# A match masked on TensorE and ScalarE in place of VectorE, and loads of a graph kernel asked for earlier

## The chip, the cores and the metric

The kernel runs on one core of one Trainium2 chip. The metric is device time in microseconds (us) of one execution; the lower the better. Five engines work in parallel, each through its own instructions in order, and meet at semaphores: TensorE (PE), VectorE (DVE), ScalarE (ACT), GpSimd (POOL) and SyncE (SP), which here only asks for transfers. A name with q (SPq, ACTq) is an engine's queue of transfer requests.

## The reference

Four graph layers run one after another over 50,000 nodes with 256 features and 50,000 edges, sorted by destination. Each layer normalizes x, rectifies it, lets nodes send messages along edges, and adds the result to x:

```python
edge_index = jnp.stack([src, dst])
h = jnp.maximum(_layernorm(x, axis=-1), 0.0)
x = x + _L0_gnn_ref(h, edge_index, L0_gnn_W, L0_gnn_b, L0_gnn_mag_w, L0_gnn_mag_b, L0_gnn_attn_w)
h = jnp.maximum(_layernorm(x, axis=-1), 0.0)
x = x + _L1_gnn_ref(h, src, dst, edge_weight, L1_gnn_w_nbr, L1_gnn_w_own, L1_gnn_bias)
h = jnp.maximum(_layernorm(x, axis=-1), 0.0)
x = x + _L2_gnn_ref(h, src, dst, L2_gnn_W_s, L2_gnn_W_t, L2_gnn_W_attn, L2_gnn_W_fc, L2_gnn_b_fc)
h = jnp.maximum(_layernorm(x, axis=-1), 0.0)
x = x + _L3_gnn_ref(h, edge_index, edge_attr_2, L3_gnn_W_forward, L3_gnn_W_reverse, L3_gnn_attn_forward)
```

Layer 0 is an attention with a softmax over the edges of a destination; layer 1 a weighted sum; layer 2 an attention with a softmax over the edges of a source, so that it needs the edges in the order of their sources; layer 3 an attention with four heads.

## The kernel before

The program is a row of stages. A stage is a `Phase`: it has its own tiles and semaphores, a block with one body for each engine, and ends with a barrier of all engines (L43), so that no work of a stage overlaps the next one's. The stages that matter here are these.

**Setup.** `constants` (L71) makes identity, ramps and `k.before`, which is 1 where the row index is smaller than the column index. `weights` (L2761) asks for 23 pieces of the weights on SyncE's queue (L2794), waits for all of them, turns them on TensorE and copies them to their places on VectorE. `load_edges` (L99) presets its tiles, asks for 24 pieces of the edge lists on SyncE's queue (L147, L148, L151), waits for all, casts them (L167), and turns them.

**Node stages** (`node_pass`, four of them, one for each layer) go over x in groups of 512 rows: SyncE loads a group, VectorE takes mean and variance and normalizes, TensorE turns and multiplies with weights, ScalarE rectifies and copies. Four buffers of x are set to zero first (L1906), and SyncE waits for that.

**Ranking** (`rank_sources`, L402, once, in layer 0) finds the place of each edge in the order of sources, a counting sort over 392 tiles of 128 edges. A source number is split in a high and a low digit. A first walk makes the histogram. The second walk, the one that the change touches, gives each edge its rank: the start of its bin, plus the earlier tiles' edges with the same key, plus those ahead of it in its own tile. For tile t:

- `head` (VectorE) makes the one-hot of the high digits, `turn` (TensorE) turns the one-hot of the low digits, `copies` (ScalarE) brings it to `low_t`.
- `match` (TensorE) multiplies `low_t` with itself: `p_same` is 1 where two edges of the tile have the same low digit, else 0. `before_in_tile` (VectorE) multiplies it by `k.before` and writes `earlier`.
- `add` (TensorE) adds the tile's counts to the running table `p_run`, in one PSUM bank. `snap` (ScalarE) copies the table to `starts` before each add. Once in eight tiles `coarsen` (VectorE) moves what has gathered to a coarse table, and a second product in `add` (L629) takes it away from `p_run`.
- `rank` (TensorE) makes three products (L647, L648 and, with `earlier`, L651), and `pick` (VectorE) picks the rank.

`walk` writes the stages of an engine's body in a fixed order with lags, the first 16 tiles straight, the others in a hardware loop with eight tiles a turn, in which the numbers to wait for and the addresses are made in registers:

```python
walk(dve, [(0, head), (2, before_in_tile), (3, coarsen), (4, pick)])
walk(pe, [(2, add), (0, turn), (1, match), (3, rank)])
walk(act, [(2, snap), (0, copies)])
```

So in step c ScalarE makes the snap of tile c - 2 and then the copy of tile c; TensorE the add of tile c - 2, the turn of c, the match of c - 1 and the rank of c - 3. A late walk (L589 to L692) follows over the last 168 tiles, with another table. Meanwhile GpSimd gathers rows of h for the edges (L732, L738, L758).

## Time and profile before

| | |
|---|---|
| time, median of 3 runs | 7717.71 us (7708.27 to 7720.84) |
| the profiled execution's own time, and its span | 7719.35 us, 7717.7 us |
| busy: TensorE, VectorE, ScalarE, GpSimd | 75%, 69%, 41%, 50% of the span |
| mean share of the 16 DMA engines | up to 9 tenths in single slices; 202 GB/s over the span |
| setup, up to the end of `load_edges` | 0 to about 54 us |
| ranking stage: histogram, walk, late walk | 672 to 842, 849 to 1374, 1374 to 1535 us |
| first clear of each node stage | 153.2, 2112.9, 3581.4, 6296.8 us |

The span runs from the first to the last instruction. Busy shares are means over stages that have different limits, so that they don't say what a stage waits for. Times in the timeline are counted from the span's start. In it, the matmuls' ends are modelled; their starts, one after another, are the better measure. An idle time in brackets names what ended it; "issue" means that nothing in the profile did.

### The profile page before, as it was taken

To read this page: it belongs to the slowest core of one execution; us is meant where nothing else is said; L and a number is where in the kernel's file an instruction comes from. 1 tells how busy PE (TensorE), PEld (TensorE's weight loads), DVE (VectorE), ACT (ScalarE), POOL (GpSimd) and SP (SyncE) were. 2 spreads that over 40 slices of the span, in tenths; PEclk is the share of its full clock that TensorE was granted. 3 is DMA by queue.
4 is the path that set the end of the run, shared out by engine and by line. 5 is a ranking of instruction groups with operands and counts; after the bars stand their busy time and mean duration, and the time that the engine had idled before them with its cause. 6 is when DMAs were issued, how large, how long until landed. Compare 5 with 4: busy or idle time off the path is not lost. (4 is left out here: it accounts for less than half of the span.)

```text
span 7717.7 us, 154759 instructions
## 1 busy us (share of the span) xinstructions
PE 5751.1 (75%) x23306; PEld 3587.8 (46%) x23307; DVE 5295.3 (69%) x18481; ACT 3154.3 (41%) x8435; POOL 3857.8 (50%) x4924
## 2 busy tenths in 40 slices
PE   4997788967789997677999877778687779400477
PEld 3774333345534444554444355555335668300365
DVE  4999888955589994456666566666784569533765
ACT  1994355214445552344444345455222457300044
POOL 1556777500022224766777677777450013577443
PEclk7998999989999998999999989998899999755799
DMA  1664334469867775797888866666108978422177
GB/s 57 212 210 144 99 103 141 139 197 326 294 226 246 244 246 192 253 308 265 313 315 314 284 199 201 204 204 204 52 25 274 338 250 230 129 55 55 49 238 250
DMA packets 917095, 1560.29 MB, mean 202 GB/s; under 512 B 122254, under 2 KB 633470, under 8 KB 916967
## 3 DMA queue, kind: packets, MB, share of 16 engines
q1 hardware_dynamic: 602758, 860.67, 33.6%
q10 hardware_dynamic: 188000, 410.91, 15.1%
q0 software_dynamic: 126208, 287.39, 13.6%
q14 instruction: 97, 0.79, 0.0%
q8 instruction: 32, 0.52, 0.0%
HBM read 861.12 MB, written 697.48 MB: 202 GB/s over the span
## 5 line engine op out<-in xcount | busy, mean ns | idle before, releaser
L2169 PE MATMUL node_p_out<-w,node_h_t 128*128 128x512 f32 (+2 forms) x6272 | 2174.6, 469 | 18.0 <-ACT node_h_t L2205 16.3
L1473 PE MATMUL merge_banks<-merge_rows,merge_mask 128*128 x6264 | 1523.3, 397 | 541.4 <-DVE merge_mask L1455 161.3
L1473 PEld LDWEIGHTS merge_banks<-merge_rows,merge_mask 128*128 128x128 f32 x6264 | 1184.6, 195 | 880.0 <-issue 723.2
L1455 DVE TENSOR_SCALAR merge_mask<-ramp,dst_at,soft_at_step 128x128 f32<-128x128 f32 x2349 | 824.7, 354 | 770.7 <-PE merge_banks L1473 613.4
L2169 PEld LDWEIGHTS node_p_out<-w,node_h_t 128*128 128x128 f32 x6272 | 1011.6, 190 | 462.8 <-issue 407.2
L2082 POOL TENSOR_TENSOR node_inv_std<-node_var,node_minus_half 128x4 f32<-128x4 f32 x392 | 461.6, 1177 | 1364.5 <-DVE node_var L1967 794.1
L1536 ACT COPY merge_total<-merge_banks 128x1024 f32<-128x1024 f32 x392 | 396.9, 1012 | 1235.7 <-PE merge_banks L1473 1215.8
L2205 ACT ACTIVATE node_h_t<-node_p_turn 128x256 f32<-128x256 f32 x1568 | 602.0, 384 | 199.9 <-PE node_p_turn L2147 194.7
L2147 PE MATMUL node_p_turn<-ident,node_xn 128*128 128x128 f32 x2352 | 466.4, 280 | 130.5 <-DVE node_xn L2038 95.6
L2147 PEld LDWEIGHTS node_p_turn<-ident,node_xn 128*128 128x128 f32 x2352 | 298.4, 141 | 454.5 <-issue 195.8
L2095 POOL DMA_INDIRECT src_sorted<-node_key,node_key_at x392 | 395.6, 1009 | 180.1 <-issue 93.7
L1524 ACT COPY merge_banks<-merge_held 128x1024 f32<-128x1024 f32 x392 | 398.4, 1017 | 193.1 <-PE merge_banks L1463 92.1
L1616 POOL DMA_INDIRECT merge_rows<-h,merge_take_i x408 | 389.5, 955 | 148.4 <-issue 104.7
L2104 POOL TENSOR_TENSOR node_small<-node_small,node_half 128x4 f32<-128x4 f32 x98 | 104.0, 1061 | 711.8 <-ACT node_junk L2184 711.8
L2409 PE MATMUL score_p_h<-w,score_h_t 128*128 128x256 f32 x1568 | 456.1, 418 | 0.1
L2336 POOL DMA_INDIRECT score_b<-to_dst,score_take_b x392 | 376.1, 959 | 119.4 <-issue 119.4
L2334 POOL DMA_INDIRECT score_a<-pair,score_take_a x392 | 377.0, 962 | 104.9 <-issue 90.1
L2546 POOL DMA_INDIRECT score_a<-h,score_take_a x392 | 375.3, 958 | 106.1 <-issue 69.0
L1453 DVE TENSOR_SCALAR merge_mask<-ramp,dst_at 128x128 f32<-128x128 f32 x783 | 297.7, 406 | 173.2 <-PE merge_banks L1473 120.6
L2221 ACT COPY node_out<-node_p_out 128x512 f32<-128x512 f32 x392 | 229.8, 586 | 435.8 <-PE node_p_out L2169 435.8
L2730 PE MATMUL head_rows_p<-ident,head_rows_cols 128*128 128x128 f32 x16 | 3.6, 423 | 523.8 <-DVE head_rows_cols L2718 523.8
L2380 DVE TENSOR_TENSOR score_z<-score_p_a,score_b 128x256 f32<-128x256 f32 x392 | 165.3, 422 | 317.8 <-ACT score_p_a L2470 301.9
(573 smaller groups left out, 11377.0 us busy)
## 6 DMA issues: line engine op xcount, KB each, us to landing
merge_held<-own ACTq DMA_DIRECT2D x196, 512.0 KB, 6.0
x<-merge_total ACTq DMA_DIRECT2D x196, 512.0 KB, 4.5
node_x<-x SPq DMA_DIRECT2D x196, 512.0 KB, 5.0
pair<-node_out SPq DMA_DIRECT2D x98, 1024.0 KB, 4.3
node_x<-in_x SPq DMA_DIRECT2D x194, 512.0 KB, 4.7
merge_rows<-h_by_edge SPq DMA_DIRECT2D x408, 128.0 KB, 3.8
merge_rows<-by_edge SPq DMA_DIRECT2D x408, 128.0 KB, 3.8
h<-node_rows_h SPq DMA_DIRECT2D x98, 516.0 KB, 4.2
```

The source lines that it names most:

```text
L1455: ins = nc.vector.tensor_scalar(mask[j][:], k.ramp[:, 0:P], columns(k.dst_at, s), columns(weight, s), ALU.is_equal, ALU.mult)
L1473: nc.tensor.matmul(banks[:, bass.ds(nc.s_assert_within(at[2 * j + 1], 0, (BANKS - 1) * 512, skip_runtime_bounds_check_because=small), D)], ...
L1524: nc.scalar.copy(four_banks(q), held[q.held][:]).then_inc(seeded, G)
L1536: nc.scalar.copy(total[q.total][:], four_banks(q)).then_inc(kept, G)
L1616: nc.gpsimd.indirect_dma_start(rows[:, (j + n) * D:(j + n + 1) * D], None, table, bass.IndirectOffsetOnAxis(take_i[:, j + n:j + n + 1], 0) ...
L2082: nc.gpsimd.tensor_tensor(inv_std[q.h][:], var[q.h][:], minus_half[:], ALU.pow).then_inc(std_made, 1)
L2095: nc.gpsimd.indirect_dma_start(k.src_sorted, bass.IndirectOffsetOnAxis(key_at[:, g:g + 1], 0), key[:, g:g + 1], None, bounds_check=k.NP - ...
L2147: ins = nc.tensor.transpose(p_turn[g % 2][:, c * P:(c + 1) * P], normal(q.h, g)[:, c * P:(c + 1) * P], k.ident[:])
L2169: ins = nc.tensor.matmul(p_out[w][g % banks][:, 0:n], h_t[g][:, c * P:(c + 1) * P], matrix[:, c, :], start=c == 0, stop=c == 1)
L2205: nc.scalar.activation(h_t[g][:], p_turn[g % 2][:, 0:D], ACT.Relu).then_inc(rectified, 1)
L2334: nc.gpsimd.indirect_dma_start(a[m][:], None, table_src, bass.IndirectOffsetOnAxis(take_a[:, m:m + 1], 0)).then_inc(got[j // LAG], 16)
L2409: ins = nc.tensor.matmul(p_h[:, 0:D], h_t[j % RING][:, c * P:(c + 1) * P], k.w2[:, c, 2 * D:3 * D], start=c == 0, stop=c == 1)
```

## The change

It has three parts. In the setup, the tiles that weights and edges are loaded to belong to a new phase `asked` that spans the first three stages; all loads are asked for in the first one, the weights on ScalarE's queue and the edges on SyncE's, and the presets of the edge tiles move there too. The node stages don't clear x. In the walk, `before_in_tile` moves from VectorE to ScalarE: a second product adds -1 to `p_same` wherever `k.before` is 0, and ScalarE takes the positive part, so that 1 is left only where the match was 1 and `k.before` is 1.

```diff
@@ constants
+            B = k.TC // P
+            nc.gpsimd.iota(e.prev_i[:], pattern=[[P * P, B]], base=-1, channel_multiplier=P).then_inc(e.preset, 1)
+            for t in e.raw_i:
+                nc.gpsimd.iota(t[:], pattern=[[P * P, B], [1, P]], base=0, channel_multiplier=P).then_inc(e.preset, 1)
...
+        @block.scalar
+        def _(act):
+            for to, frm in w.asked:
+                act.dma_start(to, frm, allow_slow_non_contiguous=True).then_inc(w.landed, 16)
+
+        @block.sync
+        def _(sp):
+            e.ask(sp)
...
+            nc.vector.memset(e.raw[2][:], 0.0).then_inc(e.preset, 1)
+            nc.vector.memset(e.pair[:], 0.0).then_inc(e.preset, 1)
@@ rank_sources
+    after_in_tile = ph.sb("after_in_tile", [P, P], F16)
...
             nc.vector.tensor_scalar(minus[:], k.ident[:], -1.0, None, ALU.mult).then_inc(negated, 1)
+            nc.vector.tensor_scalar(after_in_tile[:], k.before[:], -1.0, 1.0, ALU.mult, ALU.add).then_inc(negated, 1)
...
-            def before_in_tile(t, j):
-                dve.wait_ge(same, t + 1)
-                after(dve, ranked, t - FOUR + 1)
-                nc.vector.tensor_tensor(earlier[j % FOUR][:], p_same[j % 2][:, 0:P], k.before[:],
-                                        ALU.mult).then_inc(masked, 1)
...
-            walk(dve, [(0, head), (2, before_in_tile), (3, coarsen), (4, pick)])
+            walk(dve, [(0, head), (3, coarsen), (4, pick)])
...
-                nc.tensor.matmul(p_same[j % 2][:, 0:P], low_t[j][:], low_t[j][:],
-                                 start=True, stop=True, skip_group_check=True).then_inc(same, 1)
+                nc.tensor.matmul(p_same[j % 2][:, 0:P], low_t[j][:], low_t[j][:], start=True, stop=False)
+                nc.tensor.matmul(p_same[j % 2][:, 0:P], minus[:], after_in_tile[:], start=False, stop=True).then_inc(same, 1)
...
-            walk(act, [(2, snap), (0, copies)])
+            def before_in_tile(t, j):
+                act.wait_ge(same, t + 1)
+                after(act, ranked, t - FOUR + 1)
+                nc.scalar.activation(earlier[j % FOUR][:], p_same[j % 2][:, 0:P], ACT.Relu).then_inc(masked, 1)
+
+            walk(act, [(2, snap), (2, before_in_tile), (0, copies)])
@@ node_pass
-            sp.wait_ge(preset, S)
...
-            for h in range(S):
-                nc.vector.memset(x[h][:], 0.0).then_inc(preset, 1)
...
-            pool.wait_ge(preset, S + (2 if layer == 1 else 1))
+            pool.wait_ge(preset, 2 if layer == 1 else 1)
@@ gnn_kernel
-        constants(nc, k)
-        weights(nc, k, a)
-        load_edges(nc, k, a, sorted_rows)
+        asked = Phase(nc, "asked")
+        w, e = weight_tiles(nc, k, a, asked), edge_tiles_in(nc, k, a, asked)
+        constants(nc, k, w, e)
+        weights(nc, k, w)
+        load_edges(nc, k, e, sorted_rows)
+        asked.close()
```

`weight_tiles` and `edge_tiles_in` hold what `weights` and `load_edges` held of tiles, lists of loads and semaphores; `e.ask` waits for the five presets and then asks for the same 24 pieces as before.

## Rows read from the trace of the kernel before

**Rows 1.** Timeline of the setup stages: start, length, engine, line, idle before.
```profile
1.01 0.48 DVE L90 MEMSET pos_i<- 128x512 int32 x1 [1.01 <-PEq L2976]
...
3.89 0.46 SPq L2794 DMA_DIRECT2D weights_square<-in_L_gnn_W  x1
...
19.18 0.42 DVE L2823 TENSOR_TENSOR both_bias<-own_bias,fc_bias 128x256 f32<-128x256 f32 x1 [16.00 <-DMA weights_attn<-in_L_gnn_attn_forward]
...
28.84 0.15 DVE L2834 COPY bias<-weights_p_attn 128x2 f32<-128x2 f32 x1
...
31.44 0.33 SPq L147 DMA_DIRECT2D load_raw_i<-in_src  x1
...
42.51 0.76 DVE L167 CAST load_raw<-load_raw_i 128x512 f32<-128x512 int32 x2 [11.09 <-DMA load_prev_i<-in_dst]
```

**Rows 2.** Windows, weights load: engines busy, TensorE clock, DMA share, GB/s.
```profile
4.00:20.00 16.00, 0.80 (x4) 0.80 (x5) 0.82 (x3) 0.00 (x0) 0.00 (x0) 1.00 0.61 140
```

**Rows 3.** Timeline of the start of the first node stage.
```profile
153.20 0.91 DVE L1906 MEMSET node_x<- 128x1024 f32 x1 [3.92 <-PEq L43]
...
157.37 1.78 SPq L1868 DMA_DIRECT2D node_x<-in_x  x4
```

**Rows 4.** Instructions on tile node_x: count, shortest, median, longest in ns, starts.
```profile
L1906 DVE MEMSET node_x<- x16: 912/912/912, 153.2 to 6300.1; 128x1024 f32 x16
```

**Rows 5.** Windows, the ranking walk and the late walk behind it.
```profile
849.20:1373.60 524.40, 425.07 (x2400) 199.52 (x2400) 442.81 (x1714) 265.21 (x784) 396.82 (x489) 0.99 0.42 121
1373.60:1535.00 161.40, 155.31 (x504) 62.79 (x504) 157.04 (x681) 44.71 (x168) 82.97 (x114) 0.99 0.46 140
```

**Rows 6.** Groups by line on VectorE in the walk: busy, mean ns, idle before.
```profile
L549 DVE TENSOR_TENSOR rank_src_earlier<-rank_src_same,before 128x128 bf16<-128x128 f32 x392 | 110.2, 281 | 2.1 <-PE rank_src_same L640 0.9
```

**Rows 7.** Timeline of one even step of the walk, TensorE and ScalarE.
```profile
1100.48 0.33 PE L625 MATMUL rank_src_run<-rank_src_at_high,rank_src_at_low 128*128 128x392 bf16 x1
...
1100.64 0.22 PE L634 MATMUL rank_src_turn<-ident_bf,rank_src_at_low 128*128 128x128 bf16 x1
...
1100.74 0.22 PE L640 MATMUL rank_src_same<-rank_src_low_t 128*128 128x128 f16 x1
1100.90 0.27 ACT L685 CAST rank_src_low_t<-rank_src_turn 128x128 f16<-128x128 bf16 x1 [0.56 <-PE rank_src_turn L634]
1101.06 0.49 ACT L680 CAST rank_src_starts<-rank_src_run 128x392 f16<-128x392 f32 x1
...
1101.17 0.34 PE L647 MATMUL rank_src_rank<-rank_src_coarse,rank_src_low_t 128*128 x1 [0.21 <-ACT rank_src_low_t L685]
...
1101.51 0.33 PE L651 MATMUL rank_src_rank<-rank_src_at_high,rank_src_earlier 128*128 128x392 bf16 x1
...
1101.69 0.33 PE L625 MATMUL rank_src_run<-rank_src_at_high,rank_src_at_low 128*128 128x392 bf16 x1
```

**Rows 8.** Timeline of TensorE over the three long steps and the next.
```profile
1102.91 0.33 PE L625 MATMUL rank_src_run<-rank_src_at_high,rank_src_at_low 128*128 128x392 bf16 x1
...
1104.55 0.34 PE L625 MATMUL rank_src_run<-rank_src_at_high,rank_src_at_low 128*128 128x392 bf16 x1 [0.29 <-ACT rank_src_starts L680]
...
1106.04 0.34 PE L625 MATMUL rank_src_run<-rank_src_at_high,rank_src_at_low 128*128 128x392 bf16 x1
...
1106.38 0.22 PE L634 MATMUL rank_src_turn<-ident_bf,rank_src_at_low 128*128 128x128 bf16 x1
...
1106.45 0.22 PE L640 MATMUL rank_src_same<-rank_src_low_t 128*128 128x128 f16 x1
...
1107.51 0.33 PE L625 MATMUL rank_src_run<-rank_src_at_high,rank_src_at_low 128*128 128x392 bf16 x1
...
1107.77 0.22 PE L640 MATMUL rank_src_same<-rank_src_low_t 128*128 128x128 f16 x1
...
1108.09 0.34 PE L647 MATMUL rank_src_rank<-rank_src_coarse,rank_src_low_t 128*128 x1
```

**Rows 9.** Timeline, the last instruction of GpSimd before the late walk ends.
```profile
1489.65 0.29 POOL L718 COPY rank_src_late_src<-rank_src_of_src 128x8 f32<-128x8 f32 x1 [1.54 <-DMA rank_src_of_src<-h,rank_src_take_src]
```

More of the change, by code:

```diff
@@ L96, in constants, with edge_tiles_in @@
     ph.close()
-def load_edges(nc, k, a, rows):
-    ph = Phase(nc, "load")
-    E, TC, B = k.E, k.TC, k.TC // P
+def edge_tiles_in(nc, k, a, ph):
+    e = Asked()
+    E, B = k.E, k.TC // P
     raw_i = [ph.sb(f"raw_i{n}", [P, B, P], I32) for n in range(2)]
@@ L107, in load_edges @@
     pair = ph.sb("pair", [P, B, P, 2])
-    row_form = ph.sb("row_form", [P, B, P, 5])
-    prev_i, prev = ph.sb("prev_i", [P, B], I32), ph.sb("prev", [P, B])
-    falls, most = ph.sb("falls", [P, B, P]), ph.sb("most", [P, 1])
-    any_fall = ph.sb("any_fall", [1, 1])
-    p_falls = ph.ps("p_falls", [P, 512])
-    part = [ph.sb(f"part{n}", [P, B, P]) for n in range(2)]
-    turned = [ph.ps(f"turned{n}", [P, B * P]) for n in range(5)]
-    preset, landed, cast, turn, s_done = (ph.sem(n) for n in ("preset", "landed", "cast", "turn", "done"))
-    step, summed, rows_made, rows_put = (ph.sem(n) for n in ("step", "summed", "rows_made", "rows_put"))
+    prev_i = ph.sb("prev_i", [P, B], I32)
+    preset, landed = ph.sem("edges_preset"), ph.sem("edges_landed")
     full, rest = E // P, E % P
@@ new lines, in edge_tiles_in, with load_edges @@
+    e.raw_i, e.raw, e.pair, e.prev_i, e.preset, e.landed, e.n_landed, e.ask = raw_i, raw, pair, prev_i, preset, landed, n_landed, ask
+    return e
+def load_edges(nc, k, e, rows):
+    ph = Phase(nc, "load")
+    E, TC, B = k.E, k.TC, k.TC // P
+    raw_i, raw, pair, prev_i, landed, n_landed = e.raw_i, e.raw, e.pair, e.prev_i, e.landed, e.n_landed
+    row_form = ph.sb("row_form", [P, B, P, 5])
+    prev = ph.sb("prev", [P, B])
+    falls, most = ph.sb("falls", [P, B, P]), ph.sb("most", [P, 1])
+    any_fall = ph.sb("any_fall", [1, 1])
+    p_falls = ph.ps("p_falls", [P, 512])
+    part = [ph.sb(f"part{n}", [P, B, P]) for n in range(2)]
+    turned = [ph.ps(f"turned{n}", [P, B * P]) for n in range(5)]
+    cast, turn, s_done = (ph.sem(n) for n in ("cast", "turn", "done"))
+    step, summed, rows_made, rows_put = (ph.sem(n) for n in ("step", "summed", "rows_made", "rows_put"))
+    with nc.Block() as block:
@@ L162, in _ @@
         def _(dve):
-            nc.vector.memset(raw[2][:], 0.0).then_inc(preset, 1)
-            nc.vector.memset(pair[:], 0.0).then_inc(preset, 1)
             dve.wait_ge(landed, n_landed)
@@ L2769, in weights @@
     attn3 = ph.sb("attn3", [64, 4])
-    bias_rows = ph.sb("bias_rows", [P, 2, P])
-    spread_out = ph.sem("spread_out")
-    p_turn = [ph.ps(f"p_turn{n}", [P, 512]) for n in range(4)]
-    p_flat = ph.ps("p_flat", [P, 512])
-    p_attn = ph.ps("p_attn", [P, 512])
-    landed, turned, s_done = ph.sem("landed"), ph.sem("turned"), ph.sem("done")
+    landed = ph.sem("weights_landed")
     loads = [(square[n][:], a[name].rearrange("(d p) i -> p d i", p=P)) for n, name in enumerate(names)]
@@ L2789, in weights @@
     thin += [(attn3[:, n:n + 1], a["L3_gnn_attn_forward"][0, n:n + 1, :].rearrange("o p -> p o")) for n in range(4)]
+    w.square, w.flat, w.attn0, w.bias0, w.attn3, w.landed, w.asked = square, flat, attn0, bias0, attn3, landed, loads + thin
+    return w
+def weights(nc, k, w):
+    ph = Phase(nc, "weights")
+    square, flat, attn0, bias0, attn3, landed = w.square, w.flat, w.attn0, w.bias0, w.attn3, w.landed
+    bias_rows = ph.sb("bias_rows", [P, 2, P])
+    spread_out = ph.sem("spread_out")
+    p_turn = [ph.ps(f"p_turn{n}", [P, 512]) for n in range(4)]
+    p_flat = ph.ps("p_flat", [P, 512])
+    p_attn = ph.ps("p_attn", [P, 512])
+    turned, s_done = ph.sem("turned"), ph.sem("done")
     with nc.Block() as block:
-        @block.sync
-        def _(sp):
-            for to, frm in loads + thin:
-                sp.dma_start(to, frm, allow_slow_non_contiguous=True).then_inc(landed, 16)
         @block.tensor
         def _(pe):
-            pe.wait_ge(landed, 16 * len(loads + thin))
+            pe.wait_ge(landed, 16 * len(w.asked))
             for n in range(4):
```

38 lines of the change are left out of this document (18 added, 20 removed).

## The prediction

> **What bounds the kernel now.** One core runs its stages one after another with a barrier between them, so the time is the sum of the stages, and in each stage I ask which wait ends last. I read the timeline of the setup first, then the starts of the four node stages, then the walk of the ranking stage: windows, groups by line, and the timeline of single steps.
>
> In the setup the reader is to see two loads that nothing covers. The weights are asked for from 3.89 us and the first work on them starts at 19.18; the stage ends at 28.84. Only then are the edges asked for, from 31.44 on, and VectorE starts on them at 42.51, having waited 11.09 us [rows 1].
>
> In a node stage VectorE clears four tiles first. SyncE waits for all of them and asks for the first tile of x at 157.37, 4.17 us after the first clear began [rows 3]. There are 16 such clears, four in each of four stages [rows 4].
>
> The walk takes 524.4 us for 392 tiles, 1.338 us a tile, with VectorE busy for 442.8 us, TensorE for 425.1, ScalarE for 265.2 and GpSimd for 396.8 [rows 5]. By these shares VectorE looks like the bound, and the multiply with k.before holds 110.2 us of it [rows 6]. But the steps say otherwise. Follow one step [rows 7]: add on TensorE at 1100.48; turn at 1100.64; ScalarE's copy of what was turned at 1100.90, after 0.56 us of idleness until that turn; its snap at 1101.06, 0.49 long, so to 1101.55; and the next add at 1101.69, since add needs the snap. The next snap stands behind the next copy in ScalarE's order, and that copy needs the next turn, which stands behind this add on TensorE. This is a closed ring of 0.16 + 0.26 + 0.16 + 0.49 + 0.14 = 1.21 us, and VectorE is not in it. Five steps of eight are like it, and three are longer: 1.64, 1.49 and 1.47 us between the adds at 1102.91, 1104.55, 1106.04 and 1107.51 [rows 8]. They hold the jump back of the unrolled loop on both engines, register work behind it, and the second product of add. 5 x 1.22 + 1.64 + 1.49 + 1.47 = 10.70 us for 8 tiles, times 49 is 524.3: the ring explains the whole walk, and no VectorE instruction is needed for it.
>
> TensorE alone has nearly the same length in an even step: turn 0.16 after add, match 0.10 later, then 0.43 us without a new matmul before L647, 0.34 to L651, 0.18 to the next add [rows 7]. That gap before L647 isn't column time. I read it as the queue's own work (three waits and the address of coarse_of(t), computed in registers). It shrinks to 0.32 from 1107.77 to 1108.09 in the step where t >> 3 is already at hand [rows 8].
>
> **Setup.** The 23 weight loads go to ScalarE's queue and the 24 edge loads to SyncE's, both in the first stage. The weights can be asked for when the first stage's first instructions start, at 1.01 us [rows 1], 2.9 us earlier than 3.89. By that they would be there at 16.3. But the transfer engines were 61% busy for the 16 us of the weights' load at 140 GB/s [rows 2], that is 9.8 us of full use at 230 GB/s, and the edges, 1.0 MB by their shapes, add 4.4 us. 14.2 us of transfer from 1 us, with some 2 us of start and landing, gives 17.2; I take 17.7. From there the weights stage stays 9.8 us long, 19.18 to 28.99, and a change of stage costs about 0.9 (2.45 to the first edge load, less the two clears before it, some 1.4 by the pace of those in the node stages) [rows 1, 4], so the edges' first cast starts near 28.4, not 42.51: 14.1 us less. That the loads are then there isn't in doubt: they have some 25 us where 11 did. The added phase that holds the tiles has one more barrier, about 0.5 us. Setup: -13.6 us, between -11.5 (the loads disturb each other for 2 us more) and -15.5. On GpSimd the three iotas now stand ahead of ident and before; that is hidden under the weight loads, as are the two clears on VectorE. Without this cover they would cost 2 us.
>
> The Trainium skill (Trainium Kernel Development and Optimization, Key Constraints) says that transfers asked for by different engines run on the same 16 engines, and that spreading them saves only issue time. The trace of before, in which one queue at a time is used, doesn't show it. By that rule the gain is all from loading ahead, under other work, and none from wider transfer, as in the sum; if the transfers shared worse than that, the fourth rival below is what it comes to.
>
> **Node stages.** Each loses four clears. SyncE no longer waits and can ask for x when VectorE began to clear: 4.17 us less at most [rows 3], 4 x 0.91 = 3.65 us at least, if only the clears themselves go. I take 4.1 x 4 = 16.4 us, between 14.6 and 16.7. All of it is on the path, since the first statistics wait for that load. The wait of GpSimd for preset comes down with it and ends long before its first work.
>
> **The walk.** Removed from VectorE: 392 multiplies of 281 ns, 110.2 us [rows 6]. Worth nothing: the ring doesn't hold them. Added to ScalarE: 392 Relu of 128 columns. ScalarE's copy of 128 columns takes 0.27 us and the next instruction starts 0.16 after it [rows 7]; the Relu takes this duration too. It stands behind snap and ahead of the next copy, where ScalarE is idle for 0.56 us each step [rows 7], and its match was done on TensorE a step earlier. So it costs nothing; without that cover it would be 0.16 to 0.27 us a tile, 63 to 106 us. What is queued behind its wait is the copy, and then the snap, the ring itself, so this is the place to look.
>
> Added to TensorE: 392 products of minus with after_in_tile, 128 columns, right behind match. It delays L647, L648, L651 and so the next add, not the turn of its own step. Its price isn't in the trace. 128 columns at the pace of 392 in 0.16 us are 0.05 us. Turn and match, queued behind a full engine, start 0.07 apart at 1106.38 and 1106.45 [rows 8]; and 0.10 apart in an even step, with a wait between them [rows 7]. I take 0.06. TensorE's own length in an even step has about 0.015 us of slack (0.18 from L651 to add, of which 0.165 are columns), so four of the eight steps grow by 0.045; the fifth even step has the shorter gap, and in the three long ones TensorE waits for snap. 0.045 x 4 x 49 = 8.8 us, and one more constant on VectorE ahead of the walk costs 0.2: +9.0. The bounds are 0 (the queue's work overlaps the product) and 0.085 x 5 x 49 = 21 (0.10 each, and the jump's step grows too).
>
> The Trainium skill (TensorE: Matmul & The Clock Gate, Back-to-back issue gap) gives about 81 ns for each pair of weight load and 128-column matmul in a stream; the trace's 0.07 and 0.10 lie around it. By that figure the same sum would be 0.065 x 4 x 49 = 13 us.
>
> The late walk (161.4 us, VectorE busy for 157.0 [rows 5]) isn't edited and starts later by as much. GpSimd's gathers end at 1489.9 [rows 9], 45 us before the stage does, and stay hidden.
>
> **Sum.** -13.6 - 16.4 + 9.0 = -21.0. The profiled execution took 7719.35 us, 1.6 us more than the median of the three runs, 7717.71. So 7698.3 for an execution like it, and about **7697 us** for the median.
>
> **Rivals.**
> - **The ring takes the Relu in** (slower, 8%). If the copy is released later because the Relu in front of it still holds ScalarE or its wait, each tile pays up to 0.27 us: 7697 + 106 = 7803; it decides from 0.1 us a tile on, 39 us. For it: ScalarE is in the ring and keeps its order. Against: 0.56 us of idleness at that very place, for 0.27 [rows 7]. The Trainium skill (ScalarE: Activation LUTs, Rules for kernel authors) says to use VectorE for relu and products, not ScalarE; here that would be this rival, and the trace gives no support, as both take about 0.28 us from PSUM [rows 6, 7].
> - **VectorE was the bound** (much faster, 7%). Then the walk would fall toward TensorE's length; but GpSimd ends at 1489.9 against 1535, which caps the gain at 45: 7717.7 - 30 - 45 = 7643. For it: the highest busy share. Against: the ring closes at 524.3 without it.
> - **The product costs 0.10 in every step** (16%). 392 x 0.085 = 33 us: 7717.7 - 30 + 33 = 7721, no gain at all. Part of this case, from 21 us on, lies above my bound. For it: L647 is held by TensorE's queue, which must take one more instruction pair. Against: three steps of eight wait for ScalarE.
> - **The loads collide** (5%). The gain of the setup falls to the 2.9 us of the earlier start: 7697 + 11 = 7708.
>
> **Chances.** Forecast 64%, rivals 8, 7, 16 and 5. What a measurement can tell from no change is 0.2%, 15.4 us, so faster is below 7702.3 and slower above 7733. Forecast: 58 of 64 fall below 7702, the rest within. Third rival: 2 below, 10 within, 4 above. Fourth: within. With the others: faster 0.67, same 0.21, slower 0.12. The forecast's own range is 7685 to 7712 (sum of the bounds, -32 and -5, with the walk at 0 and +21). With cases of both signs but most of the chance near it, I widen it to 7680 to 7716; this leaves out the first two rivals and part of the third.
>
> **What would show it.** In the profile after: the first cast of the edges near 28 us, not 42.5; in each node stage the first load of x within 0.5 us of the stage's start; in the walk a window of 525 to 545 us with VectorE's busy time down by about 110 us and ScalarE's up by about 105, even steps of 1.25 to 1.27 us, the Relu between snap and copy, copy still 0.25 after turn. I am wrong if the copy starts right at the Relu's end (first rival), if the walk falls below 515 us (second), or if the long steps grow by 0.1 too (third).

## The result: 0.37% faster, and the walk did not pay for its product

| | before | after |
|---|---|---|
| time, median of 6 runs each | 7707.77 us (7703.6 to 7720.84) | 7685.3 us (7678.09 to 7693.88) |
| ratio after to before, 95% interval | | 0.9963 (0.9953 to 0.9974) |
| the profiled execution's time and span | 7719.35, 7717.7 us | 7693.88, 7692.1 us |
| busy: TensorE, VectorE, ScalarE, GpSimd | 75%, 69%, 41%, 50% | 75%, 68%, 42%, 50% |

By the ratio the change is worth 28 us (20 to 36), more than the 15.4 us that a measurement can tell from no change; the two medians are 22.5 us apart. Forecast were 7697 us and 21 us less, from a median of 7717.71 us for the kernel before, which is 7707.77 over the six runs. One execution of the node stages' edit alone, 12906.61 us at a granted clock of 0.468, was in a slow state and is left out of the ratios below.

**Setup.** The timeline of the kernel after; line numbers are its own.

```profile
0.83 0.43 ACTq L95 DMA_DIRECT2D asked_square<-in_L_gnn_W  x1
...
18.34 0.43 DVE L2851 TENSOR_TENSOR both_bias<-own_bias,fc_bias 128x256 f32<-128x256 f32 x1 [14.03 <-DMA asked_attn<-in_L_gnn_attn_forward]
...
28.03 0.15 DVE L2862 COPY bias<-weights_p_attn 128x2 f32<-128x2 f32 x1
28.89 0.43 DVE L189 CAST asked_raw<-asked_raw_i 128x512 f32<-128x512 int32 x1 [0.72 <-PEq L43]
```

The first cast of the edges stands at 28.89 us where it was at 42.51 [rows 1]; 28.4 was forecast. What ended the wait ahead of it is the barrier, not a load: the edges were there. The window of the loads shows both transfers at once (columns as in [rows 2]: length, the engines' busy time, TensorE's clock, DMA share, GB/s).

```profile
1.00:17.00 16.00, 0.00 (x0) 0.00 (x0) 2.90 (x6) 0.00 (x0) 2.79 (x7) 1.00 0.79 202
```

79% of 16 us is 12.6 us of full use, against 9.8 before, when the edges weren't in it; 14.2 was forecast. Sharing isn't free for the weights: from the first request to the first work on them 17.5 us pass, where 15.3 did. The gain is that the edges come under this wait, and no longer behind it.

**Node stages.** The start of the first one in the timeline:

```profile
140.91 0.36 SPq L1891 DMA_DIRECT2D node_x<-in_x  x1
...
140.98 0.06 DVE L1927 MEMSET node_minus_half<- 128x4 f32 x1 [3.71 <-PEq L43]
```

The first load goes out with the stage's first instructions, not 4.17 us after the first clear [rows 3].

**The walk.** Windows of the walk and the late walk, columns as above:

```profile
834.70:1349.90 515.20, 442.55 (x2783) 212.59 (x2784) 369.68 (x1316) 332.15 (x1172) 390.54 (x481) 0.99 0.41 119
1349.90:1511.00 161.10, 156.30 (x511) 63.20 (x508) 156.82 (x681) 44.55 (x168) 89.67 (x120) 0.99 0.50 152
```

515.2 us, against a forecast window of 525 to 545 and 524.4 before [rows 5]. VectorE is busy for 73 us less where 110 was forecast, and TensorE for 17 us more; ScalarE for 67 us more where 105 was forecast, since the record of the Relu begins ahead of the snap's end. An even step, TensorE and ScalarE:

```profile
1080.31 0.33 PE L643 MATMUL rank_src_run<-rank_src_at_high,rank_src_at_low 128*128 128x392 bf16 x1
1080.48 0.22 PE L652 MATMUL rank_src_turn<-ident_bf,rank_src_at_low 128*128 128x128 bf16 x1
1080.57 0.22 PE L658 MATMUL rank_src_same<-rank_src_low_t 128*128 128x128 f16 x1
1080.62 0.22 PE L659 MATMUL rank_src_same<-rank_src_after_in_tile,rank_src_minus 128*128 128x128 f16 x1
1080.73 0.27 ACT L703 CAST rank_src_low_t<-rank_src_turn 128x128 f16<-128x128 bf16 x1 [0.39 <-PE rank_src_turn L652]
1080.89 0.49 ACT L698 CAST rank_src_starts<-rank_src_run 128x392 f16<-128x392 f32 x1
1081.02 0.34 PE L665 MATMUL rank_src_rank<-rank_src_coarse,rank_src_low_t 128*128 x1 [0.18 <-ACT rank_src_low_t L703]
...
1081.27 0.30 ACT L708 ACTIVATE rank_src_earlier<-rank_src_same 128x128 bf16<-128x128 f32 x1
...
1081.53 0.33 PE L643 MATMUL rank_src_run<-rank_src_at_high,rank_src_at_low 128*128 128x392 bf16 x1
```

From add to add it is 1.22 us, as before; 1.25 to 1.27 was forecast. The product (L659) stands between the match and L665, and from the match to L665 there are 0.45 us, where there were 0.43 [rows 7]. ScalarE's idle time ahead of the copy went from 0.56 to 0.39 us: the Relu is in it, and the copy still starts 0.25 us after its turn. Now TensorE's adds over the long steps:

```profile
1073.42 0.33 PE L643 MATMUL rank_src_run<-rank_src_at_high,rank_src_at_low 128*128 128x392 bf16 x1
...
1074.97 0.34 PE L643 MATMUL rank_src_run<-rank_src_at_high,rank_src_at_low 128*128 128x392 bf16 x1 [0.20 <-ACT rank_src_starts L698]
...
1076.40 0.34 PE L643 MATMUL rank_src_run<-rank_src_at_high,rank_src_at_low 128*128 128x392 bf16 x1
...
1077.87 0.33 PE L643 MATMUL rank_src_run<-rank_src_at_high,rank_src_at_low 128*128 128x392 bf16 x1
```

They are 1.55, 1.43 and 1.47 us, against 1.64, 1.49 and 1.47 [rows 8]. So the walk's gain sits in two steps of eight, the one with the loop's jump back and the first one behind it, where I had looked for none.

In the step with the jump the difference is ScalarE's. Its copy and snap around its own jump, in the kernel before:

```profile
1103.33 0.27 ACT L685 CAST rank_src_low_t<-rank_src_turn 128x128 f16<-128x128 bf16 x1 [0.57 <-PE rank_src_turn L634]
1103.81 0.49 ACT L680 CAST rank_src_starts<-rank_src_run 128x392 f16<-128x392 f32 x1 [0.20 <-issue]
```

and in the kernel after:

```profile
1073.84 0.27 ACT L703 CAST rank_src_low_t<-rank_src_turn 128x128 f16<-128x128 bf16 x1 [0.39 <-PE rank_src_turn L652]
1074.23 0.48 ACT L698 CAST rank_src_starts<-rank_src_run 128x392 f16<-128x392 f32 x1
```

From copy to snap it is 0.48 us before and 0.39 after, with the same instructions between them (the trace has three of registers and the branch). That is the 0.09 us of the step.

**Stage by stage.** Every stage ends with a barrier, so the span can be cut there. Lengths in us, from the traces of these runs; "walk only", "setup only" and "node only" are experiments with one part of the change alone.

```
                  before   control  node only  walk only (2 runs)  setup only   after
setup               54.5      54.8       57.0       54.3  54.3         43.5      41.2
node stage 0       514.2     514.9      510.7      514.7 514.4        515.6     511.7
ranking            873.2     871.7      869.8      865.0 868.2        864.8     865.4
  its histogram    168.5     168.4      163.8      165.6 168.5        156.6     168.5
  its walk         521.4     522.1      521.7      518.4 518.7        526.0     514.9
merge 0            510.4     513.9      508.5      524.4 513.6        520.2     516.2
node stage 1       867.9     869.9      862.8      866.1 863.8        869.8     859.6
merge 1            587.9     581.8      588.1      588.6 585.6        589.8     583.4
node stage 2       848.0     849.7      845.7      853.6 853.8        851.6     842.1
shares             235.3     235.4      239.0      243.5 243.5        234.0     240.9
merge 2            523.6     521.4      526.5      520.5 520.3        523.4     527.0
node stage 3       357.0     357.0      354.8      359.3 359.1        357.0     354.7
merge 3            479.8     481.4      481.0      481.3 482.3        480.6     481.5
```

Before to after: setup -13.3, node stages -19.0, ranking -7.8, shares +5.6, all else +9.0; together -25.5, within 0.1 of the difference of the two spans. The walk here is from its first to its last add. In the setup a part is chance: the last 20 products on the weights start 0.13 us apart in some executions and 0.23 in others, 2 us in all, and the kernel of the setup only has the slower pace here, the kernel after the faster.

### The profile page after: what moved, and what is told of

It reads as the page before. It is cut to its first block and busy times, and to the rows that moved or that the text cites. A ratio compares the mean times of both kernels' runs of the same rounds, so it can differ in the third digit from the quotient of the medians.

```text
span 7692.1 us, 155635 instructions
## 1 busy us (share of the span) xinstructions
PE 5770.2 (75%) x23698; PEld 3599.3 (47%) x23699; DVE 5214.1 (68%) x18074; ACT 3216.1 (42%) x8827; POOL 3860.6 (50%) x4924
## 3 DMA queue, kind: packets, MB, share of 16 engines
q10 hardware_dynamic: 191984, 413.15, 15.3%
## 5 line engine op out<-in xcount | busy, mean ns | idle before, releaser
L2189 PE MATMUL node_p_out<-w,node_h_t 128*128 128x512 f32 (+2 forms) x6272 | 2178.8, 470 | 15.9 <-ACT node_h_t L2225 14.6
```

The lines of the kernel that those rows point to most:

```text
L2189: ins = nc.tensor.matmul(p_out[w][g % banks][:, 0:n], h_t[g][:, c * P:(c + 1) * P], matrix[:, c, :], start=c == 0, stop=c == 1)
```

## Experiments

### One part at a time, and the kernel before again

Each of these kernels holds one of the change's three parts: the diff's part in `rank_sources`, its part in `constants`, `weights`, `load_edges` and `gnn_kernel`, and its part in `node_pass`. The fourth is the kernel before, unchanged.

> The kernel before with the edit of rank_sources alone. Theory A (ring and registers: the walk is a ring through ScalarE; the Relu is hidden in its idle time, the product behind the register work ahead of L647, and the step after the jump gets shorter since a number that the snap needs is now computed at the Relu): ranking stage 7 to 8 us shorter, all of it in two of eight steps, the other six unchanged; in all -7 us. Rival B (the walk is as before or longer by my forecast, +9, and what looked like a gain came from the earlier stages or from run to run): ranking stage within 1 us of 873.2 or longer. Rival C (VectorE's relief did it): even steps shorter than 1.22 us.

> The kernel before with the edit of the setup alone. Theory: the first four stages end 13 us earlier (47.0 against 60.2 us) and all others keep their length, -13 us in all. Rival (the transfers asked for together collide so that the edges come late): less than 5 us.

> The kernel before with the edit of node_pass alone. Theory: 4.1 us for each of the four node stages, -16.4 us in all. Rival (the first loads collide with stores of the stage before, or the first group's work still waits for something else): -8 us or less. In the profile after, the four node stages were 2.6, 8.2, 5.9 and 2.2 us shorter; if these differences from 4.1 are the edit's own, this run shows them again; if they are scatter of long stages, it shows others.

> The kernel before, unchanged, as a control. Expected: ratio 1.000 within 0.1%, the setup and ranking stages within 1 us of the first profile, and the node and merge stages of some 350 to 1030 us scattered by several us, which tells how far a stage's difference between two profiles can be read.

Measured, as ratios to the kernel before with their 95% intervals: walk only 1.0020 (1.0011 to 1.0029), setup only 0.9987 (0.9978 to 0.9996), node only 0.9990 (0.9978 to 1.0002), control 1.0004 (0.9994 to 1.0013). The edited stages got shorter: the setup by 11.0 us, the node stages by 3.5, 5.1, 2.3 and 2.2 (13.1 of the 16.4 expected), the walk by 3.0, all of it in the first step behind the jump; the step with the jump kept its 1.64 us, so half of what I had expected of it is missing. But the parts don't add up: +15, -10 and -8 us make -3, and the whole makes -28: 25 us apart, where the four intervals, taken as independent, leave some 16. And the walk's edit alone made the kernel slower, although its own stage was 8.2 us shorter. In its trace the difference lies in stages that nobody edited: the shares stage took 243.5 us and not 235.3, node stage 2 took 853.6 and not 848.0. That called for more runs below. The control shows how far a stage can be read: setup, histogram, walk, shares and node stage 3 within 0.7 us of the first trace, the merges up to 6 us apart.

The setup edits alone also tell where the walk's last gain is not from: there the walk's code is that of before, and its step with the jump took 1.73 us, not 1.64. ScalarE's copy to snap across the jump took 0.56 us in it.

### Four more products

```diff
+                for _ in range(4):
+                    nc.tensor.matmul(p_same[j % 2][:, 0:P], none[:], after_in_tile[:], start=False, stop=False)
                 nc.tensor.matmul(p_same[j % 2][:, 0:P], minus[:], after_in_tile[:], start=False, stop=True).then_inc(same, 1)
```

`none` holds zeros, set once ahead of the walk.

> The changed kernel with four more 128-column products of zeros between the match and the product with minus, in each of the 392 steps of the walk; the counts are the same. Theory (the matmul pairs are issued while TensorE's queue still does its waits and register work, so a product there costs nothing): five products are 5 x 0.06 = 0.30 us at most, less than the 0.42 us that pass from the match to the turn, so even steps stay at 1.22 us, the walk at 515 us from first to last add. Rival (the prediction's price, 0.045 to 0.06 us for each product in an even step, the even steps alone): four of eight steps grow by 0.18 to 0.24 us, the walk by 35 to 47 us. Third (0.06 us in every step): +94 us.

An even step of it, TensorE's timeline:

```profile
1081.15 0.33 PE L645 MATMUL rank_src_run<-rank_src_at_high,rank_src_at_low 128*128 128x392 bf16 x1
1081.32 0.22 PE L654 MATMUL rank_src_turn<-ident_bf,rank_src_at_low 128*128 128x128 bf16 x1
1081.41 0.22 PE L660 MATMUL rank_src_same<-rank_src_low_t 128*128 128x128 f16 x1
1081.47 0.38 PE L662 MATMUL rank_src_same<-rank_src_after_in_tile,rank_src_none 128*128 128x128 f16 x4
...
1081.69 0.22 PE L663 MATMUL rank_src_same<-rank_src_after_in_tile,rank_src_minus 128*128 128x128 f16 x1
...
1081.86 0.34 PE L669 MATMUL rank_src_rank<-rank_src_coarse,rank_src_low_t 128*128 x1
...
1082.37 0.33 PE L645 MATMUL rank_src_run<-rank_src_at_high,rank_src_at_low 128*128 128x392 bf16 x1
```

Four products more, and the step is 1.22 us as before; from match (1081.41) to L669 it is 0.45 us again. The walk took 515.1 us, with 514.9 in the changed kernel, and the one execution 7690.1 us against 7714.0 of the kernel before. The products start 0.055 us apart, so the last of five starts 0.17 us ahead of L669, in the gap that is there anyway. The trace also has the queue's register instructions for L669, which the timeline leaves out: they stand at 1081.54, 1081.63 and 1081.76, two of them while the products are still starting. The theory holds, both rivals fall: a product at this place is free up to five of them at least. The Trainium skill (TensorE: Matmul & The Clock Gate, "Wait — 56ns, not 53.3ns?") says that on trn2 matmuls and weight loads are marked as issued straight to the engine, past the sequencer, and gives 55 to 56 ns from start to start at 128 columns with the clock up. The trace agrees with both: register instructions and products overlap, and the starts are 0.055 us apart at a granted clock of 1.00 (2.4 GHz). The 0.081 us for a pair, from which the prediction made its 13 us, isn't found in these six pairs.

### The Relu behind the copy

```diff
-            walk(act, [(2, snap), (2, before_in_tile), (0, copies)])
+            walk(act, [(2, snap), (0, copies), (2, before_in_tile)])
```

> The changed kernel with ScalarE's order snap, copy, Relu in the place of snap, Relu, copy. Prices the first rival of the prediction. Theory (the ring add, turn, copy, snap sets the step, and the Relu is free only because it lies in ScalarE's idle time between snap and copy): the Relu now stands between the copy and the next snap, and each step grows by 0.16 us (ScalarE's time per copy in the ring) to 0.30 us (the Relu's own duration): even steps 1.38 to 1.52, the walk from 515 to 578 to 633 us. Rival (TensorE's queue or the loop's fixed costs set the step, the ring has slack): the even steps stay within 0.03 us of 1.22.

```profile
1106.65 0.33 PE L643 MATMUL rank_src_run<-rank_src_at_high,rank_src_at_low 128*128 128x392 bf16 x1
1106.81 0.22 PE L652 MATMUL rank_src_turn<-ident_bf,rank_src_at_low 128*128 128x128 bf16 x1
...
1107.07 0.27 ACT L703 CAST rank_src_low_t<-rank_src_turn 128x128 f16<-128x128 bf16 x1 [0.56 <-PE rank_src_turn L652]
1107.23 0.28 ACT L708 ACTIVATE rank_src_earlier<-rank_src_same 128x128 bf16<-128x128 f32 x1
...
1107.40 0.49 ACT L698 CAST rank_src_starts<-rank_src_run 128x392 f16<-128x392 f32 x1
...
1108.04 0.33 PE L643 MATMUL rank_src_run<-rank_src_at_high,rank_src_at_low 128*128 128x392 bf16 x1
```

The idle 0.56 us ahead of the copy is back, the Relu pushes the snap by 0.17 us, and the step is 1.39 us. The walk took 575.0 us, 60 more, and one execution 7764.1 us against 7714.0 of the kernel before. The ring and its order are what sets the step: the same Relu costs nothing on one side of the copy and 60 us on the other.

### An idle Relu in the kernel before

VectorE still masks here; ScalarE gets one Relu more, of 40 columns, that nobody needs. In one kernel it waits as the change's Relu does, in the other without the match's count:

```diff
+            def idle(t, j):
+                act.wait_ge(same, t + 1)      # left out in the second kernel
+                after(act, ranked, t - FOUR + 1)
+                nc.scalar.activation(unused[j][:, 0:40], k.ident[:, 0:40], ACT.Relu)
-            walk(act, [(2, snap), (0, copies)])
+            walk(act, [(2, snap), (2, idle), (0, copies)])
```

> The kernel before (VectorE still masks) with one Relu more on ScalarE in each step, between snap and copy, which waits for the match's and the rank's counts as the changed kernel's does; it reads 40 columns of the identity and writes a tile that nobody reads. Theory (the first step of a block is 0.06 us shorter in the changed kernel because ScalarE works out a register number at the Relu's wait, in idle time, that before it worked out between copy and snap, in the ring): that step falls from 1.49 to 1.43 us, the even steps stay at 1.22, the walk is about 3 us shorter (518 against 521). Rival (it comes from VectorE doing one operation less, or from TensorE's two products): that step stays at 1.49.

> As the run with the idle Relu, but its Relu waits for the rank's count alone, not for the match's, so that the number for the match's count isn't worked out there. Theory (what helps is the number worked out early, not the Relu): the first step of a block stays at 1.49 us and the walk at 521 us. Rival (any operation of ScalarE between snap and copy helps): 1.43 us here too.

ScalarE in the first step behind the jump; of the kernel before:

```profile
1105.05 0.27 ACT L685 CAST rank_src_low_t<-rank_src_turn 128x128 f16<-128x128 bf16 x1 [0.76 <-PE rank_src_turn L634]
1105.31 0.49 ACT L680 CAST rank_src_starts<-rank_src_run 128x392 f16<-128x392 f32 x1
```

with the idle Relu and the match's wait:

```profile
1081.28 0.27 ACT L686 CAST rank_src_low_t<-rank_src_turn 128x128 f16<-128x128 bf16 x1 [0.63 <-PE rank_src_turn L635]
1081.47 0.48 ACT L681 CAST rank_src_starts<-rank_src_run 128x392 f16<-128x392 f32 x1
```

with the idle Relu without it:

```profile
1093.72 0.27 ACT L686 CAST rank_src_low_t<-rank_src_turn 128x128 f16<-128x128 bf16 x1 [0.63 <-PE rank_src_turn L635]
1093.98 0.49 ACT L681 CAST rank_src_starts<-rank_src_run 128x392 f16<-128x392 f32 x1
```

Copy to snap is 0.26, 0.19 and 0.26 us; the step is 1.49, 1.43 and 1.49 us, the walk 521.4, 518.6 and 523.2 us (in the last, the second step behind the jump is 0.02 us longer, too). The single executions took 7717.2 and 7720.1 us, against 7714.0 of the kernel before. In the changed kernel it is 0.19 as well (1075.48 to 1075.67) and 1.43. The snap behind that copy waits for the count 8i - 1 of adds, i being the loop's turn. In the kernel before that number is worked out between copy and snap, in the ring. The change's Relu, one place earlier, waits for the count 8i - 1 of matches: the same number, worked out while ScalarE has time. The trace has ScalarE's register instructions, which the timeline leaves out: at this place there are three between copy and snap in the kernel before and in the second kernel, and two in the first kernel and in the changed one. That is 0.06 us in one step of eight, some 3 us for the walk. An operation alone (second kernel) doesn't do it.

### Where code lies

Two kernels keep or shift the place of the code behind the ranking stage, with instructions that only count (35, 10 and 14 of them on VectorE, TensorE and ScalarE in the walk's edit alone; 17, 42 and 38 in the kernel before). The walk's edit alone was also looked at a second time, to tell chance from program.

```diff
         rank_sources(nc, k, k.pos_i, ends0, h0, score, h0_by_edge)
+        pads(nc, 35, 10, 14)
```

`pads` is a stage of its own in which the three engines do nothing but count a semaphore up so often.

> The walk's edit alone, which was 15 us slower than the kernel before although its own stage was 8 us shorter, with 35, 10 and 14 instructions that only count put on VectorE, TensorE and ScalarE right behind the ranking stage, so that the code of the later stages lies where it lay before, or 64 instructions further. Theory (the later stages' times hang on where their code lies): the stage that gives out the shares falls back from 243.5 to 235 us, the first merge from 524 to 510 to 516, the whole to 7705 to 7712 us. Rival (they differ for another reason, or by chance): the shares stay at 243 us and the whole at 7725 to 7735, or the shares are back while the rest is not.

> The kernel before with 17, 42 and 38 instructions that only count put on VectorE, TensorE and ScalarE behind the ranking stage, so that the later code lies as far on (modulo 64 instructions) as in the walk's edit alone. Theory (placing of the code): the shares rise from 235 to 243 us, the first merge from 510 to 520 or more, the whole from 7714 to 7725 to 7740 us. Rival: the shares stay at 235 us and the whole within 4 us of the kernel before.

> The walk's edit alone a second time, for one look. Theory (each program has its own times in the stages that weren't edited): the shares at 243.5 us within 1, the histogram at 165.6 us within 1, the first merge within 3 us of 524. Rival (chance from one execution to the next): the shares or the first merge off by 5 us or more; the histogram at 156.7 or 168.5.

The second look at the walk's edit alone (7725.8 us) gave 243.5 us for the shares, 853.8 and 359.1 for node stages 2 and 3, all as in the first, but 513.6 us for merge 0 where the first gave 524.4, and 168.5 for the histogram where it gave 165.6; its ranking stage was 5.0 us shorter than before, not 8.2. So merges and histogram differ by chance, by up to 11 us, and shares and node stages 2 and 3 by program. Shifted back, the walk's edit alone took 7711.6 us, ratio 0.9995 (0.9986 to 1.0004): shares 236.2, node stage 2 847.0, node stage 3 357.0. The 15 us of the walk's edit alone are gone with nothing but counting instructions added, whose own stage takes 4.3 us. The kernel before, shifted, had node stage 2 at 853.2, but the shares at 235.4; it took 7721.0 us, less than I had expected, ratio 1.0005 (0.9995 to 1.0015), with 7.2 us for the counting stage. The theory that only the place modulo 64 instructions counts is half wrong.

Then three single shifts: 29 counting instructions at the start of ScalarE's part of the ranking stage in the kernel before, 41 on VectorE at the start of the shares stage in the walk's edit alone (its place of before), and 87 there in the kernel before.

```diff
+            for _ in range(29):
+                act.sem_inc(extra, 1)
             act.wait_ge(prefix, 1)
```

> The kernel before with 29 instructions that only count at the start of ScalarE's part of the ranking stage, so that ScalarE's walk lies where it lies in the setup edits alone; the other engines' code stays where it is. Theory (the last step of a block hangs on where ScalarE's loop lies in memory): that step goes from 1.64 to 1.73 us and the walk from 521 to 526 us. Rival (another engine's position, or the loads in flight): 1.64 and 521 us.

> The walk's edit alone with 41 instructions that only count at the start of VectorE's part of the shares stage, so that VectorE's code from there on lies where it lay before; TensorE's and ScalarE's stay 48 and 44 instructions further. Theory (VectorE's place sets this stage): the shares fall from 243.5 to 235 or 236 us; the third node stage, which lies ahead of it, stays at 853. Rival (TensorE's or ScalarE's place does): the shares stay at 243.

> The kernel before with 87 such instructions at the same place, so that VectorE's code from there on lies 87 further, which is 41 back modulo 128. Theory (only the place modulo 128 instructions counts): the shares rise from 235 to 243 us. Rival (it is the place modulo 256 or more, or the distance itself): they stay near 235, or land anywhere from 230 to 250.

ScalarE's shift alone moved the walk's step with the jump from 1.64 to 1.55 us. TensorE's adds in its timeline:

```profile
1092.90 0.33 PE L626 MATMUL rank_src_run<-rank_src_at_high,rank_src_at_low 128*128 128x392 bf16 x1
1094.45 0.34 PE L626 MATMUL rank_src_run<-rank_src_at_high,rank_src_at_low 128*128 128x392 bf16 x1 [0.17 <-issue]
```

The walk took 518.5 us, 2.9 less, and ScalarE's copy to snap across the jump is 0.39 us, as in the changed kernel. I had expected 1.73 for the step: the place counts, but in the other direction, and the place of ScalarE's code alone doesn't make the 1.73 of the setup edits alone.

In the shares stage the counting instructions stand inside the stage, ahead of VectorE's first work, and take time themselves. The first instruction of VectorE in it, in the kernel before and with 87 of them:

```profile
5524.14 0.44 DVE L1731 TENSOR_SCALAR share_in_part_i<-pos_i 128x512 int32<-128x512 int32 x1 [2.28 <-PEq L43]
```

```profile
5532.54 0.43 DVE L1734 TENSOR_SCALAR share_in_part_i<-pos_i 128x512 int32<-128x512 int32 x1 [10.73 <-issue]
```

In the trace most of them are 0.093 us apart, and VectorE's first work comes 3.8 us later by 41 of them and 8.4 by 87. The stage took 238.5 us with VectorE's code back in its place, where it had been 243.5, and 251.3 with 87 in the kernel before, where it had been 235.3. Less the counting itself these are 234.7 and 242.9. The time from TensorE's first to its last turn in the stage leaves the counting out and says the same: 228.9 us in the kernel before, 237.0 in the walk's edit alone, 228.3 with VectorE back in its place, 236.1 in the kernel before with 87. So VectorE's place alone does all of it, and both theories hold: 41 back and 87 further, the same place modulo 128, cost 8.1 and 7.2 us. One such pair doesn't prove that rule. The single executions took 7727.4 and 7743.9 us, against 7710.9 of the kernel before, and 7727.6 us with ScalarE's shift. Groups by line: TensorE's turn and what it waits for, first in the kernel before, then in the one shifted by 87:

```profile
L1762 PE MATMUL share_in_turn<-ident_bf,share_in_at_low 128*128 128x128 bf16 x224 | 51.3, 229 | 25.6 <-DVE share_in_at_low L1738 22.5
```

```profile
L1765 PE MATMUL share_in_turn<-ident_bf,share_in_at_low 128*128 128x128 bf16 x224 | 51.2, 229 | 40.2 <-DVE share_in_at_low L1741 38.4
```

The same 224 instructions of the same duration; TensorE waits for VectorE's next one-hot for 38.4 us and not 22.5. Of these 15.9 us some 8.4 are the wait for the first one, behind the counting; the rest is spread over the loop, about 0.3 us in each of its 27 turns. VectorE's one-hots show where: of the eight steps of a turn six are as before, the one with the jump back takes 1.10 us and not 1.01, and one in the middle of the loop, without any jump, 1.05 and not 0.94 (1.13 and 1.07 in the walk's edit alone). The Trainium skill (Runtime: NRT & Kernel Launch, Instruction fetch mechanics) says that instructions come in blocks of 256, of which two are at hand, and that a jump outside them must fetch its block first. This fits in kind, since the same loop has another price at another place; but no run here shows the blocks, and half of the price isn't at the jump.

### Two blocks in one turn of the loop

```diff
-        with engine.Fori(2, BLOCKS) as i:
-            for j in range(U):
-                tile(i, j)
+        with engine.Fori(0, (BLOCKS - 3) // 2) as i:
+            for c in range(3 * U, 5 * U):
+                tile(c, i)
```

The first 24 tiles are straight, and `coarse_of` takes its half by a constant.

> The changed kernel with the walk's hardware loop turning every 16 steps in the place of every 8 (23 turns for 46), each half with its own constants, so that the block's parity is no register number any more. Theory (the last step of a block, 1.55 us against 1.22, is long because all queues jump back to the loop's start there, and the second step, 1.47, partly because the block's parity is worked out in registers): half of the 46 jumps go, 23 x 0.33 = 8 us, and some of the 0.25 us of the second step, 0 to 11 us: the walk from 515 to 496 to 507 us, the whole 8 to 19 us below the changed kernel (ratio to the kernel before 0.994 to 0.995). Rival (the last step is long for the work of its own stages, not for the jump): the walk stays within 3 us of 515.

```profile
834.40:1336.60 502.20, 423.65 (x2783) 216.11 (x2784) 367.08 (x1316) 328.79 (x1172) 380.51 (x466) 0.99 0.41 118
```

In this window of the walk 13 us are gone: 501.9 us from first to last add. The mean over steps of the same number is 1.43 us for the one with the jump, 1.32 for the first behind it and 1.43 for the second, where the changed kernel has 1.55, 1.42 and 1.47. These means mix two kinds. Where the loop no longer jumps, the three steps take 1.22, 1.22 and 1.38 us; where it does, 1.65, 1.42 and 1.47. So without a jump the first two are like any other step, and the jump that is left costs 0.09 us more than in the changed kernel (0.49 us from copy to snap). The time was 7679.7 us, ratio 0.9951 (0.9937 to 0.9965). That is below both kernels by its median; its interval overlaps with the changed kernel's, whose span it beats by 14.1 us, 14.3 of them in the ranking stage.

## Why the prediction came out as it did

- **Setup, -13.6: right.** Measured -13.3 at the stage's end. At the first cast it was -13.6 (28.89 for 42.51) where 14.1 was forecast, since the weights were there at 18.34, not 17.7. The change of stage was put at 0.9 us, though 2.45 less 1.4 is 1.05; it took 0.7.
- **Node stages, -16.4: near in the sum (-19.0), not stage by stage.** The first statistics come 4.5 us earlier after the stage's start (3.46 for 7.97 us in stage 0), about as costed. But "all of it is on the path" doesn't hold: at the end of stages 0 and 3 only 2.5 and 2.3 us are left of it, while stages 1 and 2 gained 8.3 and 5.9. That these make up for each other in the sum is luck. In stage 1 this is beyond chance: 863.3 to 869.9 us in twelve traces without the edit, 858.4 to 862.8 in five with it. What stage 1 gained over its 4 us, and what took the rest in stages 0 and 3, I didn't find.
- **VectorE's 392 multiplies worth nothing: right.** The ring stayed at 1.22 us without them. The walk's window of 515.2 us came to the edge of what was to be the sign against this (below 515), but the even steps didn't move, and the first step behind the jump got as short with VectorE still masking.
- **The Relu worth nothing at its place: right**, and the order test prices the first rival at 60 us.
- **The product, +8.8 us: wrong.** This is the step that failed: "TensorE's own length in an even step has about 0.015 us of slack ... so four of the eight steps grow by 0.045". I had seen the 0.43 us gap and read it as the queue's own work, and still put the product's 0.06 us on top, as if queue and array took turns. They don't: the matmul runs while the queue works on the waits behind it. Five products fit. Of my two bounds, 0 was the true one.
- **The long steps unchanged: wrong, for the better.** The first step behind the jump lost 0.06 us, by a number worked out early; the step with the jump lost 0.09, all of it on ScalarE across its jump, and a shift of ScalarE's code alone, the rest left as before, takes the same 0.09 off (0.39 for 0.48 us from copy to snap). The walk's -6.5 us is -3.0 by the first (as in the walk's edit alone) and about -3.5 by the second. That the change gets the second by the place of its code isn't shown for this kernel, but the walk's edit alone doesn't have it.
- **Stages behind the walk unchanged: wrong.** The shares stage took 240.9 us for 235.3, in the changed kernel and two variants of it alike (240.8 and 240.9). That its cost is set by where VectorE's code lies is shown for other shifts (7 to 8 us), not for this one; here, too, one step in the middle of the loop and the one with the jump got 0.11 us longer each.

The sum with what was measured: -13.3 - 19.0 - 6.5 + 5.6 = -33, within the -20 to -36 of the ratio; the other stages differ by +7.7 us between the two traces, most of it in the merges, which scatter as much in one program. That the forecast of -21 came so near is in part that three errors, +15.5 in the walk, +2.6 in the node stages and -5.6 in the shares, pull in two directions. Left open: why the change's shift costs 5.6 us in the shares, which places of a loop are dear, and what makes merge 0 differ by 11 us between two executions of one program.

## What to carry to other kernels

Before you price one more matmul on TensorE, look at what the gap behind it is: where the queue worked on waits and addresses, as here, five small products were free. On an engine inside a ring, ask on which side of the ring's own instruction an added one lies, and which register numbers it makes the engine work out early. A difference of 0.2% between two programs can lie in loops that nobody edited; cut the span at the barriers and compare stage by stage, with a second execution, before a part gets the credit or the blame. And take what a probe costs by itself off its result: here half of one shift's 16 us was the counting instructions' own time.

## What the runs showed of the hardware

- Six 128-column matmul pairs behind one another started 0.055 us apart and fitted in a gap of 0.45 us, 0.43 with one, with no change of the step.
- One register number more between two instructions of ScalarE cost 0.07 us (0.26 for 0.19 from copy to snap).
- Counting instructions put ahead of a loop, with the loop unchanged, moved the loop of the shares stage by 7 to 8 us of 229, and a step of 1.64 us by 0.09. On VectorE they take 0.093 us each themselves.
- ScalarE's copy to snap across the same loop's jump back took 0.39, 0.48 or 0.56 us in different programs, with the same instructions between them.
- The histogram, in which VectorE works beside GpSimd's gathers, took 168.5 or 156.6 us (or between) with the same code; where it was short, the gathers ended 842 to 844 us after the stage's start, where it was long at 818 to 821. The gathers' end is hidden, so the whole ranking stage is shorter where the histogram is: 858.5 and 865.0 us against 868.2 in kernels whose code is the same up to its end.
